# A 3x3 convolution's taps on TensorE: from block-diagonal 128x128 products to sixteen 32x32 tiles

## The reference

```python
h = (x - mu) * jax.lax.rsqrt(var + LN_EPS) * ln_w + ln_b
xz = jnp.einsum('bhwc,cd->bhwd', h, w_in) + b_in
x1, z = jnp.split(xz, 2, axis=-1)
y = jax.lax.conv_general_dilated(x1, conv_w, window_strides=(1, 1), padding='SAME', ...) + conv_b
return x + jax.nn.silu(y)
```

## Time and profile before

| | |
|---|---|
| median of 3 runs (lowest, highest) | 4518.78 us (4489.77, 4537.41) |
| the profiled execution, its span | 4537.55 us, 4535.8 us |
| TensorE (PE) busy, records | 3912.3 us (86%), 60188 |
| ScalarE (ACT) busy | 1810.9 us (40%) |
| VectorE (DVE) busy | 1688.8 us (37%) |
| GpSimd (POOL) busy | 223.4 us (5%) |
| mean granted TensorE clock | 0.911 |

### The profile page before, as it was taken

How to read it: one execution, slowest core, us unless ns; L and a number is a source line. 1 busy time by engine, 2 the same in 40 slices (tenths; PEclk the granted TensorE clock), 3 DMA queues, 4 the chain that set the end, 5 groups by cost and what they waited for, 6 DMA issues and landing times.

```text
span 4535.8 us, 140455 instructions
## 1 busy us (share of the span) xinstructions
PE 3912.3 (86%) x60188; PEld 2727.4 (60%) x60188; DVE 1688.8 (37%) x2829; ACT 1810.9 (40%) x3419; POOL 223.4 (5%) x489
## 2 busy tenths in 40 slices
PE   4999879988799898998989989899898998889987
PEld 2647746567456584565854757547575475664855
DVE  3323343233533335333342343423434234442343
ACT  1343344433444324443345343353433534425344
POOL 3300000000000000000000000000000000000000
PEclk8998889999999889998989989899898989989998
DMA  4201001010010100101001010010100101001000
GB/s 116 52 17 25 2 14 27 15 25 2 14 40 1 24 2 14 40 2 24 2 15 39 2 24 2 15 39 2 24 2 15 39 2 25 2 16 24 21 5 12
DMA packets 24104, 89.32 MB, mean 20 GB/s; under 512 B 17796, under 2 KB 18052, under 8 KB 19484
## 3 DMA queue, kind: packets, MB, share of 16 engines
q1 hardware_dynamic: 22179, 74.66, 6.8%
q0 software_dynamic: 1280, 5.21, 0.4%
HBM read 63.80 MB, written 14.84 MB: 17 GB/s over the span
## 4 chain that ended last, share of the span: by engine, by line
PE 77%; ACT 8%; DVE 5%; issue 5%; SPq 3%; DMA 1%; ACTq 0%; DVEq 0%
PE ps L960 77%; ACT rs L595 3%; ACT lv L590 3%; DVE area_ty L804 2%; DMA area_ty<-area_hz 1%; SPq L402 1%; SPq L419 1%; DVE xs L929 1%; ACT sq L582 1%; DVE area_ty L901 0%; DVE area_hz L899 0%; DVE area_ty L925 0%; DVE area_hz L826 0%; ACT area_ty L629 0%; SPq L403 0%
## 5 line engine op out<-in xcount | busy, mean ns | idle before, releaser
L804 DVE TENSOR_TENSOR area_ty<-ps,rs 128x448 f32<-128x448 f32 (+2 forms) x416 | 285.1, 685 | 644.3 <-ACT rs L595 644.3
L960 PE MATMUL ps<-area_ty,area_hz 113*64 113x49 f32 (+1 forms) x10240 | 413.6, 256 | 55.0 <-DMA area_ty<-area_hz 48.6
L686 ACT ACTIVATE area_ty<-ps 120x448 f32<-120x448 f32 (+1 forms) x448 | 243.6, 544 | 542.0 <-PE ps L960 542.0
L901 DVE COPY area_ty<-ps 120x448 f32<-120x448 f32 (+1 forms) x432 | 269.8, 624 | 490.8 <-PE ps L960 490.8
L686 ACT ACTIVATE area_hz<-ps 112x384 f32<-112x384 f32 (+2 forms) x384 | 191.1, 498 | 568.2 <-PE ps L960 568.2
L960 PE MATMUL ps<-g_sb,area_ty 120*96 120x56 f32 x3584 | 393.3, 285 | 26.0 <-ACT area_ty L686 13.1
L960 PE MATMUL ps<-sq,keep_sb 128*128 128x448 f32 (+1 forms) x832 | 388.2, 569 | 26.3 <-ACT sq L582 26.3
L960 PEld LDWEIGHTS ps<-area_ty,area_hz 113*64 113x64 f32 (+1 forms) x10240 | 331.8, 138 | 130.3 <-issue 126.7
L960 PEld LDWEIGHTS ps<-g_sb,area_ty 120*96 120x96 f32 x3584 | 388.8, 200 | 30.1 <-issue 30.1
L960 PE MATMUL ps<-area_ty,wconv 128*128 128x448 f32 x1008 | 398.0, 539 | 0.2
L960 PE MATMUL ps<-keep_sb,area_hz 112*56 112x56 f32 (+1 forms) x12288 | 374.4, 225 | 13.2 <-DVE area_hz L899 13.2
(11 more groups left out here) (107 smaller groups left out, 4450.6 us busy)
## 6 DMA issues: line engine op xcount, KB each, us to landing
area_hz<-f_all SPq DMA_DIRECT2D x16, 2541.0 KB
xw<-x_in SPq DMA_DIRECT2D x8, 1568.0 KB, 6.8
y_out<-xs SPq DMA_DIRECT2D x32, 294.0 KB
f_all<-piece POOLq DMA_DIRECT2D x16, 317.6 KB, 4.2
area_ty<-area_hz SPq DMA_DIRECT2D x256, 4.6 KB
area_hz<-raw_in SPq DMA_DIRECT2D x1, 2894.0 KB, 9.9
g_sb<-g_in SPq DMA_DIRECT2D x2, 1396.5 KB
g_sb<-g_in SPq DMA_DIRECT2D x1, 1470.0 KB
```

Source lines behind the costliest of these rows:

```text
L686: act.activation(dst, src, ACT.Relu if st in (ST_H, ST_F2) else ACT.Copy).then_inc(sc_kept, 1)
L804: ve.tensor_tensor(o, a, b, ALU.mult, **kw).then_inc(normed, 1)
L901: ins = ve.tensor_copy(dst, src)
L960: return pe.matmul(o, a, b, start=start, stop=stop)
```

## The change

Each tap of an image is now a product of a 32x32 matrix with 392 positions (7 rows). The picture is cut into two halves of 28 rows (`GROUPS`), a half into four chunks of 7 rows. For one tap of one half TensorE issues sixteen such products: image j (partitions 32j of `pad` and of the weights) by chunk c (PSUM partitions 32c), into bank 4g+j. PSUM then has the chunk on partitions and the image on banks ("chunk order"). Silu runs in that order, on two banks at once (784 columns), in place in `yc`. Sixteen products with a 32x32 identity carry it back to PSUM with the image on partitions and the chunk on banks, and VectorE adds it from there to `xs` in four additions of 392 columns per half.

The order of work changes too. All seven `LN_CONV` tiles are normed in one row; the first half's taps wait for tiles 0 to 3, and tiles 4 to 6 are normed between its taps. ScalarE has no convolution work between norming steps any more: it norms all seven, takes silu of half 0, norms `LN_MIX(0)` tiles 0 to 2, takes silu of half 1, norms tiles 3 to 6. VectorE follows the same order. PSUM banks of both LNs move, still two each.

```diff
-                for s in range(CONV_SLOTS):
...
+                for i in range(NT):
+                    if i + 1 < NT:
+                        square(q, LN_CONV, i + 1)
+                    invert(q, LN_CONV, i)
+                for g in range(GROUPS):
+                    k = (q * GROUPS + g) * 2
+                    act.wait_ge(conved, q * GROUPS + g + 1)
...
+                    first, end = MIX_OF[g]
+                    square(q, LN_MIX(0), first)
+                    for i in range(first, end):
+                        if i + 1 < end:
+                            square(q, LN_MIX(0), i + 1)
+                        invert(q, LN_MIX(0), i)
...
-            for j in range(QI):
-                su(ve.tensor_scalar(wconv[:, :, j, :],
-                                    ps[:, 5, 0:9 * RW].rearrange("p (t n) -> p t n", t=9),
-                                    R("block")[:, j:j + 1], None, ALU.mult))
+            su(ve.tensor_copy(wconv[:, :, :], ps[:, 5, 0:9 * RW].rearrange("p (t n) -> p t n", t=9)))
...
+                def tap(g, n):
+                    dy, dx = n // 3, n % 3
+                    pe.sem_inc(passed_pe, 1)
+                    for c in range(CHUNKS):
+                        h = GROUP_ROWS * g + CR * c + dy
+                        for j in range(QI):
+                            r = slice(RW * j, RW * j + RW)
+                            ins = mm(ps[RW * c:RW * c + RW, 4 * g + j, 0:CW].rearrange("p (h w) -> p h w", w=HW),
+                                     wconv[r, n, :], pad[r, h:h + CR, dx:dx + HW], start=n == 0, stop=n == 8)
...
+                def move(g):
+
+                    pe.wait_ge(silued, (q * GROUPS + g + 1) * 2)
+                    pe.sem_inc(passed_pe, 1)
+                    for c in range(CHUNKS):
+                        r = slice(RW * c, RW * c + RW)
+                        for j in range(QI):
+                            ins = mm(ps[RW * j:RW * j + RW, 4 * g + c, 0:CW], ident[r, r], yc[r, g, j, :])
+                        ins.then_inc(conv_moved, 1)
...
                 center_conv(0)
                 center_conv(1)
+                pe.wait_ge(mlp_added, q * NW + NW)
+                for i in range(LAST_OF[0] + 1):
+                    variance(q, LN_CONV, i)
+                    center_conv(i + 2)
                 pe.wait_ge(border, q + 1)
+                pe.wait_ge(normed, ln_count(q, LN_AT[LN_CONV, LAST_OF[0]]))
+                tap(0, 0)
+                tap(0, 1)
+                variance(q, LN_CONV, 4)
+                center_conv(6)
+                tap(0, 2)
+                variance(q, LN_CONV, 5)
+                tap(0, 3)
+                tap(0, 4)
+                variance(q, LN_CONV, 6)
+                for n in range(5, 9):
+                    ins = tap(0, n)
+                ins.then_inc(conved, 1)
+                pe.wait_ge(normed, ln_count(q, LN_AT[LN_CONV, LAST_OF[1]]))
+                for n in range(6):
+                    tap(1, n)
+                move(0)
+                tap(1, 6)
+                tap(1, 7)
+                center_mix(0)
+                center_mix(1)
+                variance_mix(0)
+                tap(1, 8).then_inc(conved, 1)
+                center_mix(2)
+                variance_mix(1)
+                variance_mix(2)
+                move(1)
+                center_mix(3)
+                center_mix(4)
+                for i in range(3, NT):
+                    variance_mix(i)
+                    if i + 2 < NT:
+                        center_mix(i + 2)
```

More of the change, by code:

```diff
@@ L84, in LN_FFN @@
     return 4 + 2 * l
-CONV_SLOTS = NT + 1
+GROUPS, GROUP_ROWS = 2, HW // 2
+CHUNKS = 4
+CR = GROUP_ROWS // CHUNKS
+CW = CR * HW
+LAST_OF = [3, NT - 1]
+MIX_OF = [(0, 3), (3, NT)]
 FFN_SLOTS = NT + 3
@@ L96, in _tile_order @@
     order = [(LN_WIN2, i) for i in range(NW)] + [(LN_CONV, 0), (LN_CONV, 1)]
-    for s in range(CONV_SLOTS):
-        order += [(w, i) for w, i in ((LN_CONV, s + 2), (LN_MIX(0), s - 1)) if 0 <= i < NT]
+    order += [(LN_CONV, i) for i in range(2, NT)] + [(LN_MIX(0), i) for i in range(NT)]
     for l in range(2):
@@ L654, in conv @@
                 square(q, LN_CONV, 0)
[L655 to L668, removed]
-                                       bias=act_bias[:, 0:1]).then_inc(neg_exped, 1)
-                        act.wait_ge(neg_exped, k + 1)
-                        act.activation(ln1, en, ACT.Ln, bias=act_bias[:, 1:2]).then_inc(log1ped, 1)
-                        if s >= 1:
-                            act.wait_ge(silued, k)
-                        act.wait_ge(log1ped, k + 1)
-                        act.activation(sg, ln1, ACT.Exp, scale=-1.0).then_inc(sigmoided, 1)
-                    if s >= 1:
-                        invert(q, LN_MIX(0), s - 1)
@@ L1129, in center_conv @@
                     center(q, LN_CONV, i, xs)
-                def taps(i, first, end):
-                    for tap in range(first, end):
-                        dy, dx = tap // 3, tap % 3
-                        ins = mm(ps[:, 6 + i % 2, 0:TT].rearrange("p (h w) -> p h w", w=HW),
-                                 wconv[:, tap, :, :].rearrange("p j n -> p (j n)"),
-                                 pad[:, TR * i + dy:TR * i + dy + TR, dx:dx + HW],
-                                 start=tap == 0, stop=tap == 8)
-                    return ins
+                def tap(g, n):
[7 more added lines that the diff above has]
+                                     wconv[r, n, :], pad[r, h:h + CR, dx:dx + HW], start=n == 0, stop=n == 8)
+                    return ins
@@ L1146, in conv @@
-                for s in range(CONV_SLOTS):
-                    if s + 2 < NT:
-                        center_conv(s + 2)
-                    if s < NT:
-                        pe.wait_ge(normed, ln_count(q, LN_AT[LN_CONV, min(s + 1, NT - 1)]))
-                        if s >= 2:
-                            pe.wait_ge(silued, q * NT + s - 1)
-                        taps(s, 0, 5)
-                    if s >= 1:
-                        pe.wait_ge(conv_added, q * NT + s)
-                        center(q, LN_MIX(0), s - 1, xs)
-                    if s + 2 < NT:
-                        variance(q, LN_CONV, s + 2)
-                    if s < NT:
-                        taps(s, 5, 9).then_inc(conved, 1)
-                    if s >= 1:
-                        variance(q, LN_MIX(0), s - 1)
+                pe.wait_ge(normed, ln_count(q, LN_AT[LN_CONV, LAST_OF[0]]))
```

72 lines of the change are left out of this document (44 added, 28 removed).

## The result

| | before | after |
|---|---|---|
| median (lowest, highest) of 20 runs each | 4521.16 us (4489.77, 4541.09) | 4542.22 us (4514.25, 4564.02) |
| ratio, 95% interval | | 1.005 [1.003, 1.007] |
| span of the profiled execution | 4535.8 us | 4562.3 us |
| mean granted TensorE clock | 0.911 | 0.880 |
| TensorE busy in the eight stages, summed | 570.9 us | 423.3 us |

The change costs 21 us, half a percent. I had forecast a gain of 0.3%. The time lies inside the range, and both numbers are within the 1% that I had called no change, but the sign is wrong: with 20 runs each the interval leaves out 1.000. Two terms of the sum turn out to be off, and a third part had been left out of it.

A forecast was written before the change was run, and what follows sets the result against it. Taps' throughput plus a latency chain bound the old stage, the norm chain the new: 70.9 + 7.2 = 78.1 us per quad, 1.3 less; with `wconv`, 12 us less in all, 4507 us median, range 4445 to 4575.

The forecast's parts named there:

- the clock's term: Thin stretches of the convolution stage run partly at the lower clock: 7.2 us per stage, half of the bounds 0 and 15.
- the tap: Sixteen 32x32 products of 392 columns advance together on TensorE: 0.70 us per tap at full clock, 1.4 as other bound.
- a norming tile in the front: Before the first tap, `LN_CONV` tiles run one behind another, each costing 3.81 us.
- silu of half 0 starts: After half 0's taps, ScalarE starts its silu 29.4 us behind the first centering, at full clock.
- silu of half 1 starts: ScalarE norms `LN_MIX(0)` tiles 0 to 2 first, so this silu starts at 47.9 us, at full clock.
- the mixer starts: End of the stage's path at full clock: 70.9 us from the first centering, 8.5 less than 79.4.
- What bounds the stage: In the new convolution stage, the layer norm's chain sets the length; 33 us less TensorE work per quad buys 8.5 us.
- Outside the stage: Other queues issue and wait as before; beyond the stages only making `wconv` was counted, at most 1.6 us less.
- the clock lies low on the whole chain: Rival: every thin pair in the stage pays for the lower clock, 85.9 us per stage, 4569 us in all; chance 16%.
- The rival of the clock held up: Clock stays at its upper level in the stage: each stage 8.5 us less, 4449 us in all; chance 22%.
- Idle TensorE ahead of the second move: Sign: TensorE stands idle for 8 us before the convolution stage's second move.
- PE's sum of busy time down by over 200 us: Sign for the taps: TensorE's summed busy time falls by over 200 us.

The follow-up runs named there:

- the kernel whose clock was held up: The changed kernel plus products nobody reads where TensorE waits: after the first four variances, before the second move, after late variances; 4397.17 us, 0.977 of the kernel before.

## Why the prediction was wrong

The step that failed is the clock's term: "rows 9 show both levels in turn, so I take half", 7.2 us per stage. It measured 9.6 us, and the parts outside the stage, which the sum left alone, moved too. A second, smaller failure is the tap. Point by point, times from the first centering, at the upper level; what was measured is from the windows of the kernel whose clock was held up:

| | summed | measured |
|---|---|---|
| a norming tile in the front | 3.81 | 3.79 |
| first tap (15.4 + 0.77 + 0.75 + 0.1) | 17.0 | 17.03 |
| silu of half 0 starts | 29.4 | 31.25 |
| silu of half 1 starts | 47.9 | 49.34 |
| the mixer starts | 70.9 | 71.42 |
| clock's penalty, mean of eight | 7.2 (0 to 15) | 9.6 (6.9 to 13.6) |
| the stage | 78.1 | 81.0 |

- **What bounds the stage** was read rightly: the chain of norms and silus, not TensorE's work. Taking 148 us of TensorE's busy time out of the eight stages bought nothing.
- **The tap** failed: 0.88 us for 0.70. The bound by issue (0.51 us) was taken as no matter, since it is less than the stream. What failed is the rule that the larger of two bounds is the time; with the two this near it isn't. It cost 1.9 us up to silu of half 0, of which 1.3 were given back by links that came out shorter (from silu of half 1 to the mixer 23.0 was summed and 22.1 measured).
- **The clock** failed in size, and that made the sign. I had seen that thin stretches lose the clock and taken half of the bound, 7.2 us. Three quads paid 13.6 us, near the bound, and five 6.9 to 7.5, which is the half; that I took one number for two kinds of stage is the error. With the 0.5 us of the links it makes 81.0 - 78.1 = 2.9 us per stage, 23 us in all, and turns -1.3 into +1.6 per stage. Why three quads lose the clock earlier in the front than the other five (5.4 us for 9.7 behind the first centering) and for longer stays open.
- **Outside the stage** I had allowed for nothing. The first mixers' +6.7 us go with their clock, and so, it seems, do some 8 us in the norm and MLP ahead of the stage, whose low-clock time rises by 9 and 11 us; no run isolates these. The rival *the clock lies low on the whole chain* came nearest in time (4569 us). Its 85.9 us per stage is what three quads show (85.05); the other five, at 78.3 to 78.9, show the forecast's 78.1. That the total fell between the two is no merit of either.
- **The rival of the clock held up** was right in its mechanism and its price. It gave 4449 us, and with the clock made to hold in the stages, the kernel ran at 4397. The rival priced the stages alone, 68 us (59 measured, 576.25 for 634.98); the first mixers gave another 54 (729.19 for 782.91).
- **Signs to look for.** Tap of 0.70 us: 0.88. First tap at 15 to 17 us: 22 and 19, since the low clock stretched it. Idle TensorE ahead of the second move: 7.62 us for 8. Mean clock below 0.911: 0.880. PE's sum of busy time down by over 200 us: 127, since a record at the lower level counts up to twice, the taps were slower, and drains count in short records; how much each of these gives was not measured. Making `wconv` is 0.459 us for 2.1.

TensorE's timeline shows the idle time ahead of the second move, in the changed kernel's first quad:

```profile
307.72 1.62 PE L965 MATMUL ps<-area_ty,ident 32*32 32x392 f32 x32 [7.62 <-DVE area_ty L885]
```

## What to carry to other kernels

When a change takes work off TensorE, price the cover that goes with it: count the chain that lay under the work, and read what clock a stretch as thin as the new one was granted. Then give the chain room first (here two lists of PSUM banks, 0.970) before paying for the clock with work that nobody reads (0.951 with both). And compare against the old kernel with the same care: idle products at the end of its stage took the old taps to 0.988 as well, 9 us of it in the stages and 48 in the mixers behind them.

## What was not expected of the hardware

- Unread products make a kernel faster: 576.25 us in place of 647.99 for the same stages, with 47 us more of TensorE busy time in them (470.4 for 423.3).
- Sixteen 32x32 float32 products of 392 columns take 0.88 us, eight 0.63, sixteen of 168 columns 0.51.
- The same 1857 records of a mixer take 89.5, 91 to 92, 95.8 or 98.6 us, two or more of these in one execution, by where in them the clock falls. One of the falls comes while TensorE is busy, with no idle time above 0.9 us in the 25 us ahead of it; its cause is open. A stage far from a change can so move the total by more than the change does: the first mixers alone span 716.04 to 789.64 us over these kernels.
